# Attention added to x by accumulating transfers from GpSimd's queue, and h scaled and anchored in two halves of 704 columns

## The reference

```python
x = x + xattn(layernorm(x), ctx, ctx, Wq, bq, Wout, bout)
x = x + ffn(layernorm(x), w_gate, w_up, w_down)

def xattn(Q, K, V, ...):
    # q, k, v = projections to 16 columns; corr = circular correlation of q and k,
    # averaged over batch and channel; the 12 best shifts, softmax over them;
    # R = sum of w_i * roll(v, -shift_i); the same R for all 16 heads; R @ Wout + bout
def fp4_linear(x, w):
    return jnp.einsum('bsk,nk->bsn', fp4_quant_dequant(x), fp4_quant_dequant(w))
gate = fp4_linear(x, w_gate); y = fp4_linear(x, w_up)      # 256 -> 704
h = silu(gate) * y
return fp4_linear(h, w_down)                               # 704 -> 256
```

## Time and profile before

| | us |
|---|---|
| median of three runs | 575.65 |
| the profiled execution's own time | 575.05 |
| its span (first to last instruction) | 573.2 |
| PE busy | 466.7 |
| DVE busy | 461.9 |
| ACT busy | 393.3 |
| POOL busy | 282.7 |

### The profile page before, as it was taken

One profiled execution on the slowest core, in us unless ns is written; L12 is line 12 of the kernel. 1 busy time (PEld: TensorE's weight loads), 2 busy tenths in 40 slices (PEclk: granted clock), 3 DMA queues, 4 the chain that ended last, 5 costly groups with the idle time before them and its releaser, 6 DMA issues. The chain is left out here.

```text
span 573.2 us, 10039 instructions
## 1 busy us (share of the span) xinstructions
PE 466.7 (81%) x3454; PEld 306.1 (53%) x3454; DVE 461.9 (81%) x742; ACT 393.3 (69%) x666; POOL 282.7 (49%) x365
## 2 busy tenths in 40 slices
PE   5086798704789999999899999999899999999944
PEld 5075687501345565556555555556555565556633
DVE  2899864315799999999899999999899999998760
ACT  2177865535778777788888777788888778776530
POOL 3045351035356666656556666656556666632221
PEclk9689999775989999999999999999999999999987
DMA  9956550043145556555655557645655556544533
GB/s 283 344 170 202 176 186 14 25 102 75 37 97 122 110 122 127 120 106 111 128 118 119 110 123 126 121 107 110 130 116 119 112 115 110 108 88 98 88 78 78
DMA packets 165042, 69.19 MB, mean 121 GB/s; under 512 B 129152, under 2 KB 164736, under 8 KB 164992
## 3 DMA queue, kind: packets, MB, share of 16 engines
q1 hardware_dynamic: 164416, 68.03, 52.2%
q10 hardware_dynamic: 576, 0.53, 0.3%
HBM read 27.90 MB, written 9.18 MB: 65 GB/s over the span
## 5 line engine op out<-in xcount | busy, mean ns | idle before, releaser
L694 PE MATMUL ps<-guT_hi,a_xT 128*128 128x512 f16 (+1 forms) x384 | 140.7, 366 | 55.2 <-DMA a_xT<-ctx_sb 55.2
L405 POOL TENSOR_TENSOR ctx_sb<-h_c,sl 128x704 f16<-128x704 f16 x64 | 96.1, 1523 | 115.8 <-DVE ctx_sb L909 115.8
L704 PE MATMUL ps<-dT_hi,hqT 128*128 128x256 f16 x704 | 132.2, 276 | 12.3 <-DMA hqT<-ctx_sb 12.3
L696 PE MATMUL ps<-guT_hi,a_xT 128*128 128x512 f16 (+1 forms) x384 | 140.3, 365 | 0.0
L695 PE MATMUL ps<-guT_lo,a_xT 128*128 128x512 f16 (+1 forms) x384 | 140.1, 365 | 0.0
L694 PEld LDWEIGHTS ps<-guT_hi,a_xT 128*128 128x128 f16 x384 | 37.7, 98 | 103.7 <-DMA a_xT<-ctx_sb 46.0
L457 ACT ACTIVATE h_c<-y_h 128x1408 bf16<-128x1408 bf16 (+3 forms) x40 | 49.2, 1230 | 61.9 <-DVE y_h L939 36.5
L706 PE MATMUL ps<-dT_lo,hqT 128*128 128x256 f16 x384 | 89.6, 277 | 0.0
L704 PEld LDWEIGHTS ps<-dT_hi,hqT 128*128 128x128 f16 x704 | 69.7, 99 | 25.2 <-DMA hqT<-ctx_sb 13.1
L443 POOL TENSOR_TENSOR xs<-xs,w_raw 128x512 f32<-128x512 f32 x32 | 37.8, 1180 | 79.5 <-issue 49.6
L904 DVE SCALAR_TENSOR_TENSOR hb<-ps,h_in,w_raw 128x704 f32<-128x704 f32 x64 | 60.5, 945 | 4.7 <-PE ps L696 4.6
(11 more groups left out here) (139 smaller groups left out, 868.8 us busy)
## 6 DMA issues: line engine op xcount, KB each, us to landing
w_raw<-a_scratch SPq DMA_DIRECT2D x64, 128.5 KB, 2.6
xs<-in_x_dram SPq DMA_DIRECT2D x16, 512.0 KB, 5.3
ctx_sb<-in_ctx_dram SPq DMA_DIRECT2D x16, 512.0 KB, 4.4
out_dram<-a_xT SPq DMA_DIRECT2D x64, 128.0 KB, 2.0
hqT<-ctx_sb SPq DMA_TRANSPOSE x64, 3.7
w_raw<-in_L_ffn_w_down_dram SPq DMA_DIRECT2D x1, 704.0 KB, 8.1
w_raw<-in_L_ffn_w_gate_dram SPq DMA_DIRECT2D x1, 640.0 KB, 5.9
w_raw<-in_L_ffn_w_up_dram SPq DMA_DIRECT2D x1, 640.0 KB, 7.1
```

The lines of the kernel that those rows point to most:

```text
L405: pool.tensor_tensor(hq[:, j % 2, t, FF:2 * FF].rearrange("p (ih r) -> p ih r", ih=IH), h_c[:, :].bitcast(F16).rearrange("p (ih t r) -> p ...
L694: pe.matmul(dst, xt[:, c, :], guT[0][:, c, n0:n1], start=(c == 0), stop=False)
L696: last = pe.matmul(dst, xt[:, KC + c, :], guT[0][:, c, n0:n1], start=False, stop=(c == KC - 1))
L704: pe.matmul(dst, hqT[:, j % 4, c, :], dT_hi[:, c, :], start=(c == 0), stop=False)
```

## The change

1. The attention is no longer loaded to a buffer and added by GpSimd. GpSimd issues 17 accumulating transfers (`add_attn`: two of one pair, fifteen of two pairs, 1028 contiguous numbers per partition), which add the attention and minus its mean right into `xs`, which now has 257 columns a batch. `a_scratch` is laid out so that one partition's part of several batches is contiguous. The loads on SP and lines 443 and 444 go. From step -4 every even step issues one, for the pairs that ACT squares two steps later.
2. `y_h` is done in two instructions of 704 columns, and `split` on h in two halves, each of which waits only for its half of y_h. The buffer `h_c` of the anchor is double (`h_c[j % 2]`).
3. The block maxima of x are taken for pair st+3 after y_x, where they were taken for pair st+2 ahead of the scales; `xn` has two buffers, and ACT's normalization and sum of squares run one pair further ahead, as do GpSimd's statistics.
4. `low_h` is done in two places: tile 0 at the start of GpSimd's step, tile 1 after `sl`, with a wait until y_x of pair st+2 is done. SP's order becomes turn_h, turn_x, turn_h.
5. `s32` (line 428) goes: the factor 2^11 moves into the constants, so that `sl` is formed from bm itself.

```diff
-K_H, K_HQ, K_XQ, K_W, K_R = 3, 4, 5, 4, 3
+K_H, K_HQ, K_XQ, K_W, K_R = 3, 5, 5, 4, 3
-FIRST, END = -5, NP + 4
+FIRST, END = -4, NP + 4
+SUMS = (1, 1) + 15 * (2,)
-        a_dram = nc.dram_tensor("a_scratch", [B * ROWS8, DA], F32, kind="Internal").ap()
-        xs = sb("xs", [P, B, D])
+        a_dram = nc.dram_tensor("a_scratch", [ROWS8, B * DA], F32, kind="Internal").ap()
+        xs = sb("xs", [P, B, DA])
...
# SP
-                    turn_h(2 * st - 4)
-                    turn_h(2 * st - 3)
-                if pair_ok(st + 1):
-                    turn_x(st + 1)
+                    turn_h(2 * st - 4)
+                if pair_ok(st + 1):
+                    turn_x(st + 1)
+                if pair_ok(st - 2):
+                    turn_h(2 * st - 3)
-                if pair_ok(st + 6) and st + 6 >= 2:
-                    load_attn(st + 6)
...
# GpSimd
+            def add_attn(k):
+                n0 = sum(SUMS[:k])
+                if n0 % (NP // 4) == 0:
+                    pool.wait_ge(a_io[n0 // (NP // 4)], 16)
+                row, cols = 2 * n0 * DA, 2 * SUMS[k] * DA
+                pool.dma_start(xs[:, 2 * n0:2 * (n0 + SUMS[k]), :].rearrange("p t n -> p (t n)"),
+                               bass.AP(a_dram.tensor, row, [[0, HEADS], [B * DA, ROWS8], [1, cols]]), accum_op=ALU.add
+                               ).then_inc(s[f"x1_in{k}"], 16)
...
             for st in range(FIRST, END):
                 if pair_ok(st - 2):
-                    low_h(st - 2)
-                n = st + 3
+                    low_h(st - 2, 0)
+                n = st + 4
...
-                    pool.tensor_scalar(s32[:, n0:n1], bm[:, 1, n0:n1], X_SCALE * DOWN, 1.0, ALU.mult, ALU.mult).then_inc(s["s32"], 1)
-                    pool.wait_ge(s["s32"], m + 1)
...
-                    x1 = xs[:, 2 * n:2 * n + 2, :]
-                    pool.tensor_tensor(x1, x1, attn[:, n % 2, :, 0:D], ALU.add)
-                    pool.tensor_tensor(s_nm[:, n % 2], neg_mean[:, 2 * n:2 * n + 2], attn[:, n % 2, :, D], ALU.add
-                                       ).then_inc(s["x1_done"], 1)
+                if pair_ok(st - 2):
+                    if pair_ok(st + 2):
+                        pool.wait_ge(s["x4_steps"], K_XQ * (st + 2) + 1)
+                    low_h(st - 2, 1)
+                if st + 6 >= 2 and st + 6 < NP and st % 2 == 0:
+                    add_attn(st // 2 + 4)
...
# ScalarE
-                j, n, b = st - 1, st + 2, st + 3
+                j, n, e, b = st - 1, st + 2, st + 3, st + 4
...
-                    act.wait_ge(s["x1_done"], b + 1)
+                    act.wait_ge(s[f"x1_in{sum_of(b)}"], 16)
...
-                    act.wait_ge(s["h4_steps"], K_HQ * j + 1)
-                    need(act, s["loh"], 2 * j)
-                    split(h_t[:, :], h_c[:, :], y_h[:, :], s["h_split"], 3 * j)
+                    need(act, s["loh"], 2 * (j - 1))
+                    for k in range(2):
+                        half = slice(FF * k, FF * (k + 1))
+                        act.wait_ge(s["h4_steps"], K_HQ * j + 1 + k)
+                        split(h_t[:, half], h_c[j % 2][:, half], y_h[:, half], s["h_split"], 6 * j + 3 * k, X_SCALE)
...
# VectorE
-                if pair_ok(xb):
-                    dve.wait_ge(s["xn_ready"], xb + 1)
-                    dve.tensor_reduce(bm[:, 0, RUN_H:NS], xn.rearrange("p (b i) -> p b i", i=BLK), AX.X, ALU.max,
-                                      apply_absolute_value=True).then_inc(s["x_max"], 1)
...
-                    dve.tensor_tensor(y_h[:, :].rearrange(runs, ih=IH, il=2), hb[:, :].rearrange(runs, ih=IH, il=2),
-                                      bm[:, 2, 0:RUN_H].unsqueeze(1).unsqueeze(3).broadcast_to([P, IH, 2 * NBH, 2]), ALU.mult
-                                      ).then_inc(h4, 1)
+                    for k in range(2):
+                        half = slice(FF * k, FF * (k + 1))
+                        need(dve, s["h_split"], 6 * (j - 1) + 3 * k + 3 if j else 0)
+                        dve.tensor_tensor(y_h[:, half].rearrange(runs, ih=IH // 2, il=2), hb[:, half].rearrange(runs, ih=IH // 2, il=2),
+                                          bm[:, 2, 0:RUN_H].unsqueeze(1).unsqueeze(3).broadcast_to([P, IH // 2, 2 * NBH, 2]), ALU.mult
+                                          ).then_inc(h4, 1)
...
+                if pair_ok(st + 3):
+                    dve.wait_ge(s["xn_ready"], st + 4)
+                    dve.tensor_reduce(bm[:, 0, RUN_H:NS], xn[:, (st + 3) % 2, :].rearrange("p (b i) -> p b i", i=BLK), AX.X, ALU.max,
+                                      apply_absolute_value=True).then_inc(s["x_max"], 1)
                 if tile_ok(2 * st):
                     gate_up(2 * st)
```

More of the change, by code:

```diff
@@ L157, in build @@
         bm = sb("bm", [P, 3, NS])
-        s32 = sb("s32", [P, NS])
         sh = sb("sh", [P, 2, 2 * NS], BF16)
@@ L192, in build @@
             "w_loaded", "small_loaded", "late_loaded", "x_loaded0", "x_loaded1", "x_loaded2", "x_loaded3",
-            "c_loaded0", "c_loaded1", "c_loaded2", "c_loaded3", "attn_loaded0", "attn_loaded1",
+            "c_loaded0", "c_loaded1", "c_loaded2", "c_loaded3", *(f"x1_in{k}" for k in range(len(SUMS))),
             "stored0", "stored1", "stored2", "stored3", "consts", "w_steps", "w_pool", "w_lo", "w_hi", "w_split", "root_set", "w_tr", "w_ev",
@@ L220, in runs_of, with sum_of @@
             return w[:, FF * (g % 2):FF * (g % 2) + n].rearrange("p (ih c r) -> p c ih r", ih=IH, r=r)
+        def sum_of(n):
+            return next(k for k in range(len(SUMS)) if n < sum(SUMS[:k + 1]))
         def pair_ok(n):
@@ L315, in _ @@
             sp.dma_start(cT[:, :], bass.AP(w_dram.tensor, P, [[2 * P - 1, P], [1, P]])).then_inc(s["t_io"], 16)
[L317 to L324, removed]
             def turn_h(i):
@@ L397, in _, with low_h @@
                     w_lo(i - W_FIRST - 2)
-            def low_h(j):
+            def add_attn(k):
[6 more added lines that the diff above has]
+                               ).then_inc(s[f"x1_in{k}"], 16)
+            def low_h(j, t):
                 pool.wait_ge(s["h4_steps"], K_HQ * (j + 1))
                 pool.wait_ge(s["sl"], j + 1 - SC0 + 1)
[L402 to L409, removed]
+                need(pool, hT[2 * (j % 2) + t], 16 * (j // 2))
+                pool.tensor_tensor(
+                    hq[:, j % 2, t, FF:2 * FF].rearrange("p (ih r) -> p ih r", ih=IH),
+                    h_c[j % 2][:, :].bitcast(F16).rearrange("p (ih t r) -> p t ih r", ih=IH, t=2)[:, t],
+                    sl[:, (j + 1) % 2, t * RUN_H:(t + 1) * RUN_H].unsqueeze(1).broadcast_to([P, IH, RUN_H]),
+                    ALU.mult).then_inc(s["loh"], 1)
+            pool.wait_ge(s["trx"], 2 * NQ)
+            for k in range(2):
+                add_attn(k)
             for st in range(FIRST, END):
                 if pair_ok(st - 2):
-                    low_h(st - 2)
-                n = st + 3
+                    low_h(st - 2, 0)
+                n = st + 4
                 if pair_ok(n):
@@ L452, in w_hi, with split @@
                 act.activation(chunks_of(w_q[0], g), runs_of(hb, g), ACT.Copy).then_inc(s["w_hi"], 1)
-            def split(t, c, y, done, at):
+            def split(t, c, y, done, at, unit):
                 top = high_half(y).bitcast(BF16)
-                act.activation(c.bitcast(BF16), top, ACT.Square, scale=ANCHOR_SLOPE).then_inc(done, 1)
-                act.activation(t.bitcast(F16), top, ACT.Copy, scale=STICKY).then_inc(done, 1)
+                act.activation(c.bitcast(BF16), top, ACT.Square, scale=ANCHOR_SLOPE * unit).then_inc(done, 1)
+                act.activation(t.bitcast(F16), top, ACT.Copy, scale=STICKY * unit).then_inc(done, 1)
                 act.wait_ge(done, at + 1)
@@ L468, in w_split @@
                     act.wait_ge(s["root_set"], 1)
-                split(h_t[:, 0:n], h_c[:, 0:n], y_h[:, 0:n], s["w_split"], 3 * g)
+                split(h_t[:, 0:n], h_c[0][:, 0:n], y_h[:, 0:n], s["w_split"], 3 * g, 1.0)
             def evac_x(i, u):
@@ L537, in _ @@
                     for t in range(2):
-                        last = act.activation(sq_out[:, t, :], xs[:, 2 * b + t, :], ACT.Square, bias=s_nm[:, b % 2, t:t + 1],
+                        last = act.activation(sq_out[:, t, :], xs[:, 2 * b + t, 0:D], ACT.Square, bias=xs[:, 2 * b + t, D:DA],
                                               accum_out=s_sq[:, b % 2, t:t + 1])
@@ L561, in _ @@
                     act.wait_ge(s["x4_steps"], K_XQ * n + 1)
-                    split(x_t[:, :], x_c[:, :], y_x, s["x_split"], 3 * n)
+                    split(x_t[:, :], x_c[:, :], y_x, s["x_split"], 3 * n, X_SCALE)
         @block.tensor
@@ L776, in stats_a @@
                 for t in range(QT):
-                    last = dve.bn_stats(a_bst[:, i % 2, t, :], xs[:, QT * i + t, :])
+                    last = dve.bn_stats(a_bst[:, i % 2, t, :], xs[:, QT * i + t, 0:D])
                 last.then_inc(s["stats"], 1)
```

74 lines of the change are left out of this document (32 added, 42 removed).

## The result

The changed kernel takes 705.3 us (704.03 to 707.38), where the kernel before took 576.3 us in the same runs. The ratio is 1.223, 95% interval 1.217 to 1.228: it is 22% slower, where 552.5 us was forecast. The profiled execution has a span of 702.2 us against 573.2.

A forecast was written before the change was run, and what follows sets the result against it. No engine was full; the loop y_h on DVE, ACT's anchor, offset on DVE set 12.91 us a step. 27 x (12.91 - 12.08) = 22.4, + 0.9 + 0.9 - 1.2 = 23.0 off 575.05; as median 552.5 us, range 546 to 564.

The forecast's parts named there:

- DVE's step: DVE's work per second-phase step: 12.03 us by the sum, 12.08 with 0.05 for waits between halves, from 12.91.
- offset and grid on x: DVE's two instructions on x, no longer beside GpSimd's L434: from 0.50 + 0.74 to 0.41 + 0.42 us, -0.41.
- ACT's six activations: ACT's split of h in halves of 704 columns: 4.37 us for 4.00 before.
- The anchor: ACT's anchor of h: done 10.09 us after the h multiplication starts, with DVE reaching offset at 10.15.
- PE's wait for x's transposition: PE waiting for the transposed x, with turn_x issued 0.9 us earlier: from 1.18 us to 0.1 to 0.3.
- the one on the transfers: Accumulating transfers of 514 KB every second step: wanted 15 us after issue, so hidden and costed at nothing.
- 10.6 us as upper end: Landing time of the accumulating transfer: 2.6 to 10.6 us, the upper end from the 5.3 us load read twice.
- Rival 4: Transfers land too late for the square two steps on: slower from 16.5 us, about 596 us at 18; chance 0.06.
- Rival 2: The transfer's issue on GpSimd takes over 2.6 us and pushes the first low_h: 565 us in the middle; chance 0.08.
- Rival 1's contention: ACT's activations not overlapping, or GpSimd's statistics blocking L932: steps 12.3 to 12.4 us, about 561 in all; chance 0.20.
- The first last instruction of a step: Start of the second phase, ACT's squares and normalization reordered: together +1.2 us, from -1.5 to +4.
- The three last steps: End of the second phase: 0.3 us gained each, -0.9 in all (+1.5 to -2.1).

The follow-up runs named there:

- e1: Changed kernel without its 17 accumulating transfers, so the attention is not added to x: 552.69 us, ratio 0.959.
- e4: Changed kernel with accumulating transfers of one pair, issued every step right after sl: 559.52 us, ratio 0.968; again 557.26 us, ratio 0.965.
- e5: Changed kernel with its two-pair transfers every second step issued right after sl: 564.01 us, ratio 0.975; again 563.72 us, ratio 0.976.
- e7: e4 with both multiplications of low_h at the start of GpSimd's step again: 576.6 us, ratio 0.999 to the kernel before.
- e2: Changed kernel with the same 17 transfers as plain copies that overwrite x instead of accumulating: 577.8 us, ratio 1.001.

## Why the prediction was wrong, by its own steps

**What held.** DVE's step of 12.03 to 12.08 us is 12.12 in most undisturbed steps. Its terms: offset and grid on x 0.41 and 0.43, scales 0.28, the second low_h from 8.84 to 10.36 us into the step (8.7 to 10.3 forecast), the issue 0.91 us and harmless, ACT's six activations 4.37 us (313.06 to 317.43), begun 0.14 us later than reckoned: the first half of y_h takes 1.07 us for the 0.99 reckoned, and ACT's scaling of the output ahead of them, itself 0.52 us late by PE, ends only at 313.09. The anchor ends at 10.23 where 10.09 stood, DVE comes at the same moment. The forecast's total without the transfers, 552.5 us, is near e1's 552.69, in part by luck: from the first to the last h multiplication e1 gains 20.5 us over before (378.8 for 399.3) where 24.2 were forecast, and it begins them 4.3 us sooner (154.18 for 158.45), with no transfer to wait for, where 1.2 later was forecast. PE's wait for x's transposition goes down as said.

**The step that failed** is the one on the transfers: "so all of 2.6 to 10.6 is hidden and I cost it at nothing". It asked only when the transfer lands for its own reader, and priced the transposition beside it, "landed by 3.7 us at 14.0; PE wants it at about 14.5", from a row where nothing from another queue was in flight. The two facts that it needed stood in the text a few lines apart: the second low_h ends at 10.3, the transposition is issued at 10.3, the transfer right behind low_h, and PE can wait 0.5 us. What each does to the other was never asked. The runs show in its place: 11.2 us on the transposition (14.7 for 3.5) and 8.7 on the transfer (14.3 for 5.6), every second step, 12 long steps that are on average 12.4 us over 12.12, together 149 us. The spans of the changed kernel and of e1 differ by 702.2 - 548.8 = 153.4.

**The bound.** 10.6 us as upper end, twice a plain load, is no bound for a transfer that meets a transposition: it took 14.3. Alone it takes 5.6, near the nearest row's 5.3.

**The rivals.** Rival 4 had the sign and a size, 596 us at 18 us, but the wrong place. ACT never waits for x1_in in the steady steps although the transfers take 13.2 to 16.1 us, around the 14.8 from which it was to decide; the steps had become longer. The time goes to a bystander. Rival 2 fell: the issue takes 0.91 us. The Trainium skill's warning of stalled descriptors ("SBUF — State Buffer", section "SBUF: two separate sides") is not what happened: in e4 the issue lies beside y_h and the transfer lands in 4.4 us. The estimate of 3.2 us for 514 KB from the Trainium skill, "DMA: Bandwidth & Descriptors", section "Anatomy of one DMA — SWDGE (gpsimd) path", is short of the 5.6 measured in e5. Rival 1's contention was a few hundredths.

**Smaller terms.** The first last instruction of a step comes at 160.37 for 158.45, +1.9 where +1.2 was taken: the first square starts 0.9 us sooner (121.36 for 122.24) and the third waits 1.16 us for the first transfer of two pairs. The three last steps take 37.3 us, a gain of 0.3 for 0.9: one of them is 13.45, where the second low_h, which nothing holds back, lies on y_h (its halves take 3.22 us for 1.87). Two readings of the prediction are off without moving its result: 552.1 and 0.6 make 552.7 and not 552.5, and the grid instruction of the earlier trace rows ends 0.28 us after L434, not 0.42; that the two engines take turns is seen better in e7.

**What stays open** is why the accumulation makes both so slow. DMA engines that take turns between queues packet by packet are the obvious account, and the packets in the traces don't bear it out. A transfer of two pairs is 128 packets of 4112 bytes, 8 for each of the 16 engines, most of them 0.33 us long: 2.6 us. The transposition's 1408 packets of 256 bytes take 1.9 us an engine in e1. One behind the other these are under 5 us. In e2 it looks like that: the copy's packets run from 273.3 to 276.2, most of the transposition's follow from 275.5. In the collision shown above both crawl instead: the transfer's packets start between 319.68 and 330.97 and last up to 3.7 us, and from 320.5 to 323.25 some 160 transposition packets start, where alone 200 start in 0.25 us. What holds them the runs don't show. In e4 the packets hardly meet: the even tile's transposition moves its own from 311.5 to 313.3, the transfer from 314.4 to 317.2, x's transposition from about 317.1. So what an accumulating transfer does to a transposition that is already half moved was not tried.

## What to carry to other kernels

Price a new transfer at what it does to the transfers that are already in flight at that moment: list every queue's issues and landings over one period, put the new one in the gap, and cut it to the gap's length. A semaphore or an instruction that releases two queues at once is the place to look first; here moving the issue from behind the second low_h to ahead of it is worth 140 us. Ahead of a chain with a slack of 0.5 us no cost from an unshared row may stand in for a shared one.

## What the runs showed of the hardware that was not expected

- A transposing transfer and an accumulating one in flight together cost far more than one after the other: 14.3 and 14.7 us for 5.6 and 3.5. The Trainium skill, "SBUF — State Buffer", section "Can I just issue two DMAs to hit both halves?", has two concurrent transfers at only 6% over a single one and says that they serialize; a sum of 9.1 us would be the worst of that here. The measurement decides: for an accumulating transfer beside a transposition it is not so. A copy beside one, 5.1 and 6.0 us, stays within it.
- A plain copy of the same bytes at the same moment costs the transposition 2.5 us in the median (6.0 for 3.5, up to 8.8), the accumulating one 11.5.
- SP's queue is held with it: issues that take 0.4 and 1.4 us take up to 3.1 and 7.4 us while accumulating transfers and transpositions are in flight.
- An accumulating transfer away from transpositions is not slow: 257 KB in 4.4 us (e4), 514 KB in 5.6 (e5), the plain load of 512 KB in 5.3.
